# Self heads over fewer score banks: transposed scores on two PSUM banks, a value bank for each group, two buffers of reciprocals

## The reference, cut to what matters

```
# L0 and L3: gated memory
memory_proj = memory @ W_mem
attn = softmax(hidden @ memory_proj^T / sqrt(D));  context = attn @ memory_proj
gate = sigmoid([hidden, context] @ W_gate + b);    out = rmsnorm(hidden + gate * context)

# L1, self attention: the part that the change touches
x = rms_norm(hidden, ln_in_w)
mixed = where(vm, x @ v_qkv, x @ l_qkv)            # q, k, v: 16 heads of 16 features
q, k = apply_rotary(q, k, position_ids)
ctx = softmax(q k^T / 4, causal) @ v
hidden = hidden + where(vm, ctx @ v_dense, ctx @ l_dense)
...                                                # cross attention, experts
```

## Time and profile before

| | |
|---|---|
| median of 3 runs | 784.29 us (783.54 to 785.41) |
| the profiled execution | 783.74 us, its span 781.9 us |
| PE busy | 695.7 us (89%) |
| DVE, ACT, POOL busy | 408.9, 354.2, 107.1 us |
| mean granted TensorE clock | 0.938 |
| DMA | 34.55 MB, mean 44 GB/s |

### The profile page before, as it was taken

How to read it: one execution, slowest core, us unless ns; L and a number is a source line. 1 busy time by engine, 2 the same in 40 slices (tenths; PEclk the granted TensorE clock), 3 DMA queues, 4 the chain that set the end, 5 groups by cost and what they waited for, 6 DMA issues and landing times.

```text
span 781.9 us, 13323 instructions
## 1 busy us (share of the span) xinstructions
PE 695.7 (89%) x5560; PEld 547.7 (70%) x5560; DVE 408.9 (52%) x814; ACT 354.2 (45%) x702; POOL 107.1 (14%) x140
## 2 busy tenths in 40 slices
PE   7698898789999899999886969977899999999995
PEld 5576675547987677689774857754497967667984
DVE  2637826645764745252356394375655756443424
ACT  3503253466442466554253124524664335665424
POOL 0100000362000132300001000005700002332000
PEclk9989999688999999999997988987799999999998
DMA  7042000020103000050400020000220400000000
GB/s 287 20 178 81 2 2 29 1 75 21 55 21 142 1 2 1 1 189 1 168 27 1 1 81 2 2 28 1 75 74 2 156 7 1 1 2 1 1 0 28
DMA packets 6843, 34.55 MB, mean 44 GB/s; under 512 B 1536, under 2 KB 3072, under 8 KB 5248
## 3 DMA queue, kind: packets, MB, share of 16 engines
q1 hardware_dynamic: 5344, 26.85, 9.3%
q10 hardware_dynamic: 1440, 6.86, 2.4%
HBM read 32.66 MB, written 1.05 MB: 43 GB/s over the span
## 4 chain that ended last, share of the span: by engine, by line
PE 73%; DVE 18%; ACT 6%; issue 2%; DMA 0%; DVEq 0%; ACTq 0%; SPq 0%
PE ps_A L898 4%; PE ps_B L898 4%; PE ps_A L683 4%; PE ps_B L683 3%; PE ps_B L861 3%; PE ps_A L861 3%; PE ps_B L975 2%; PE ps_B L696 2%; PE ps_A L696 2%; PE ps_A L975 2%; DVE max_B L1620 2%; PE ps_A L1025 2%; PE ps_B L1025 2%; PE ps_A L1013 2%; PE ps_B L1013 2%; PE ps_A L649 2%
## 5 line engine op out<-in xcount | busy, mean ns | idle before, releaser
L1620 DVE TENSOR_REDUCE max_A<-ps_A 128x2 f32<-128x512 f32 x64 | 40.2, 685 | 21.6 <-PE ps_A L824 12.1
L1620 DVE TENSOR_REDUCE max_B<-ps_B 128x2 f32<-128x512 f32 x64 | 40.4, 685 | 20.3 <-PE ps_B L824 11.4
L544 POOL TENSOR_TENSOR xv_B<-big_B 128x256 f32<-128x256 f32 x24 | 18.5, 778 | 226.0 <-ACT big_B L1302 113.1
L544 POOL TENSOR_TENSOR xv_A<-big_A 128x256 f32<-128x256 f32 x24 | 17.6, 743 | 209.2 <-ACT big_A L1306 107.8
L861 PE MATMUL ps_B<-q_B,kz_B 64*128 64x256 f32 (+1 forms) x320 | 33.4, 315 | 7.2 <-ACT big_B L1306 4.0
L1137 ACT ACT_TABLE_LOAD x29 | 37.2, 1283 | 0.5
L861 PE MATMUL ps_A<-q_A,kz_A 64*128 64x256 f32 (+1 forms) x320 | 32.8, 315 | 5.0 <-ACT big_A L1306 4.2
L861 PEld LDWEIGHTS ps_B<-q_B,kz_B 64*128 64x128 f32 (+1 forms) x320 | 24.3, 197 | 17.6 <-ACT big_B L1306 7.0
L683 PE MATMUL ps_B<-q_B,kz_B 128*128 128x256 f32 x264 | 36.2, 299 | 0.5 <-DVE kz_B L1532 0.3
L683 PEld LDWEIGHTS ps_B<-q_B,kz_B 128*128 128x128 f32 x264 | 34.3, 202 | 2.6 <-issue 1.4
L683 PE MATMUL ps_A<-q_A,kz_A 128*128 128x256 f32 x264 | 35.1, 295 | 1.1 <-DVE q_A L1511 1.1
(11 more groups left out here) (379 smaller groups left out, 1693.2 us busy)
## 6 DMA issues: line engine op xcount, KB each, us to landing
ffn_w<-in_l1m SPq DMA_DIRECT2D x2, 3072.0 KB, 11.1
ffn_w<-in_l2f SPq DMA_DIRECT2D x2, 3072.0 KB, 10.7
attn_w<-in_l1a SPq DMA_DIRECT2D x2, 2048.0 KB, 10.5
v_B<-in_l1d ACTq DMA_DIRECT2D x2, 1408.0 KB, 6.1
v_A<-in_l1d ACTq DMA_DIRECT2D x2, 1408.0 KB, 5.9
attn_w<-in_l2q SPq DMA_DIRECT2D x2, 1024.0 KB, 5.2
attn_w<-in_l2q SPq DMA_DIRECT2D x4, 512.0 KB, 4.9
v_A<-in_gm SPq DMA_DIRECT2D x2, 512.0 KB, 5.0
```

The lines of the kernel that those rows point to most:

```text
L544: nc.gpsimd.tensor_tensor(L.key_sums(a, i), p[:, 0:S], p[:, S:2 * S], ALU.add)\
L1620: last = nc.vector.tensor_reduce(mx[:, :, h], L.ps[:, h % 4, :].rearrange("p (q k) -> p q k", q=ST), AX.X, ALU.max)
```

## The change

For self heads `SCORE_BANKS` goes from 3 to 2: a pair of transposed scores now waits for both exponentials of the pair before it. `value_bank` gives the first group bank 2 and the second bank 3, so that `busy` is 2 and no `weigh` waits for `head_out` of the group before. `recip` gives each group a half of `L.xn`. Beside that the table `ORDER` is another one for all four engines. The number of instructions is the same on every engine.

```diff
@@ ORDER @@
     "PE": [
-        2, 2, 2, 2, 1, 1, 1, 1, 2, 2, 1, 1, 2, 1, 1, 8, 6, 1, 1, 3, 1, 2, 1, 4, 2, 1, 1, 1, 2, 1, 1, 3, 2,
+        2, 2, 2, 2, 1, 1, 1, 1, 2, 2, 1, 1, 2, 1, 1, 8, 5, 1, 2, 3, 1, 2, 1, 2, 2, 2, 2, 1, 1, 1, 2, 1, 1,
...
@@ -421,14 +421,14 @@
-        SCORE_BANKS = [3, 3, 2]
+        SCORE_BANKS = [2, 3, 2]
 
         def value_bank(a, g):
 
-            return 2 + g % 2 if a == LATENT else 3
+            return 3 if a == CROSS else 2 + g % 2
 
         def recip(L, a, g):
-            return L.chunk(L.probs, g % 2) if a == LATENT else L.recip[:]
+            return L.chunk(L.probs, g % 2) if a == LATENT else L.chunk(L.xn, g) if a == SELF else L.recip[:]
@@ -880,7 +880,7 @@
-                        busy = 2 if a == LATENT else 1
+                        busy = 1 if a == CROSS else 2
```

More of the change, by code:

```diff
@@ L137 @@
     "PE": [
[10 rows of a table removed]
-    "ACT": [
[6 rows of a table removed]
-    "DVE": [
[6 rows of a table removed]
[10 rows of a table added]
+    "ACT": [
[6 rows of a table added]
+    "DVE": [
[6 rows of a table added]
     "POOL": [
-        0, 1, 2, 17, 16, 8, 8, 9, 9, 1, 17, 16, 8, 8, 8, 8],
+        0, 1, 2, 17, 16, 8, 8, 9, 9, 1, 11, 2, 2, 1, 2, 3, 2, 10, 8, 8, 8, 8],
 }
```

## The result

The changed kernel takes 804.49 us (median of 4 runs, 802.26 to 806.66) against 784.18 (783.54 to 785.41): ratio 1.027, 95% interval 1.024 to 1.030, 20.3 us slower. The forecast was 794.3 with a range up to 802. The sign was right, the size was not, and the time lies outside the range. The profiled execution took 806.66, its span is 804.9. The four executions stand in two pairs, 802.26 and 802.59 at a mean granted clock of 0.934, 806.38 and 806.66 at 0.922, and the profile is of the second pair.

What follows compares the result with a forecast made beforehand. The prediction took TensorE, busy 89% of the span, to bound the kernel. Its terms, 7.7 + 0.3 + 4.5 + 1.0 − 3.5 = +10.0 us, gave 793.7 for the profiled execution, 794.3 against the median, range 784 to 802.

Steps and rivals of the forecast that it cites:

- Value banks and reciprocals: Self heads' weigh and reciprocal: freed of waiting for head_out, where nothing was lost; gain 0, at most 0.3 us.
- The context load: Between the passes: PE reaches L592 sooner, but ctx_B lands no earlier behind ffn_w; 7.7 us of new idle.
- third rival: Between the passes: the small context load lands early, as ctx_A did, so no 7.7 us wait; 786.6 us, chance 0.08.
- Between the passes, the rest: Norms, rotary, clock and stacking between the passes, beside the load: sum +0.3 us, between −6 and +5.
- The rotary's 3.5: Between the passes: DVE does lane B's rotary between lane A's norms, so A's L664 waits; +3.5 us.
- the clock's 1.5: Between the passes: the long idle lets the clock fall, so one or two products more run at half rate; +1.5 us.
- The 2.3 of A's gated memory: Between the passes: DVE and ACT finish lane A's gated memory during the load's wait, so its waits go; −2.3 us.
- The second wait for the keys' casts: Between the passes: the lanes' stacking comes singly, giving a second wait like the one before; +2.9 us.
- Second pass, self attention: All 32 heads' maxima precede the first transposed scores, so DVE bounds the stage; +4.5 us, bounds −2 and +9.
- First pass, self attention: Two pairs of A's maxima ahead of B's last two delay B's first transposed scores; +1 us, −2 to +4.
- Cross and latent attention: Both passes: closer lanes put one's pairs over the other's 0.68 us waits; −3.5 us, bounds −7 and +2.
- second rival: Self attention: two score banks cost more than the order covers, half of 64 pairs uncovered, 14 us; 802.6 us, chance 0.11.

Runs made afterwards that it cites:

- e2: The changed kernel's banks (two for scores, value bank per group, two reciprocals) with the table ORDER of the kernel before; 787.03 us.
- e1: The changed kernel, with SyncE issuing lane B's context for the second pass ahead of the ffn_w load; 795.19 us.
- e8: The kernel before with two score banks for self heads alone, value bank, reciprocal and table as before; 788.73 us.
- e3: The kernel before with the new table ORDER alone, so three score banks, one value bank, one reciprocal; 807.10 us.
- e9: The kernel before, three score banks, with the new table up to the end of the first pass and the old one after; 789.30 us.
- e10: The kernel before, three score banks, with the new table throughout and lane B's context issued ahead of ffn_w; 792.70 us.
- e4: The changed kernel's banks, with the old table up to the end of the first pass and the new one after; 801.26 us.
- e6: The changed kernel's banks and the old table, with the new table only from the stacking before the second pass's self attention on; 799.09 us.
- e7: The changed kernel's banks, new table only from first pass's end to stacking of the second's self heads, lane B's context ahead of ffn_w; 802.28 us.
- e5: The changed kernel's banks, with the new table up to the end of the first pass and the old one after; 784.45 us.
- e11: The kernel before with the new table only up to the first steps of the first pass's self attention; 781.65 us.

## Why the prediction was wrong

By its steps, on the profiled executions (+23.0 us of span, forecast +10.0):

- **Value banks and reciprocals, 0.** Right; L898 doesn't wait for DVE in either kernel, and e2 shows no cost of its own for them.
- **The context load, 7.7.** Right in mechanism and size: 7.9 in the trace, and 7.2 to 9.3 with the half clock behind it by e1. The chance for the third rival (the load lands early) was rightly small, 11.1 us against 2.1.
- **Between the passes, the rest, +0.3.** Too small in the sum, 1.3 us more idle beside the load and 1.8 of clock, and right only in some of its parts. The rotary's 3.5 came as the 3.3 at L696, the clock's 1.5 as 1.8. A's norm waits went by 3.2 and B's grew, not the 5.3 that I credited. The 2.3 of A's gated memory did not go: L633 and L649 still wait 1.6, and L611 and L623 3.3 beside them. The second wait for the keys' casts (+2.9) did not come: there is one, now of lane B, 3.3 in place of 2.9.
- **Second pass, self attention, +4.5.** Measured 2.3 idle and 2.0 of clock, 4.3 in all. DVE bounds the maxima as said, but PE waits 5.8 us for them and not some 10, and the term had no clock in it. The near hit is partly luck.
- **First pass, self attention, +1.** Measured 1.5 idle and 1.4 of clock, but not for the reason given. The stage idles 10.8 to 11.0 us in every trace with two banks, with the old table too (e2, e8), and 9.2 to 9.8 in every trace with three, with the new table too (e3, e9, e10). So the idle is the banks' and not that of A's maxima put ahead.
- **Cross and latent attention, −3.5.** This is the step that failed, and with it the range. From the first cross attention to the experts' end and from the second to the end of the kernel the changed kernel idles 3.3 us more and loses 3.7 to the clock, +7.0 in place of −3.5: 10.5 of the 13 us missed. In e1, whose clock was the better, the same rows give 4.3 us more idle and 1.7 less of clock, still +2.6. I argued that closer lanes cover each other's waits for exponentials. They cover 0.7 us of them: in the two cross stages these waits came to 7.9 us before and 7.2 in the changed kernel. I had set the term from 24 us of idle without asking how much of it was such waits. What grew is waits for DVE. PE's waits in the first pass's cross stage, before (134 to 245 us) and changed (134 to 262 us):

```profile
PE ps_A L861 <- ACT big_A L1306: 2.5, 3, 1.1
PE ps_B L861 <- ACT big_B L1306: 1.1, 2, 0.7
PE ps_B L809 <- DVE max_B L1620: 0.7, 1, 0.7
PE ps_B L683 <- DVE q_B L1511: 0.2, 1, 0.2
```

```profile
PE ps_B L809 <- DVE max_B L1620: 2.8, 3, 1.7
PE ps_A L861 <- ACT big_A L1306: 2.6, 3, 1.2
PE ps_B L683 <- DVE q_B L1511: 2.0, 1, 2.0
PE ps_B L861 <- ACT big_B L1306: 0.9, 2, 0.7
```

The first of these, lane B's wait for its maxima, is the new table's: 2.6 to 2.8 us in all six traces that have it in the first pass, 0.7 or less in the ten others. The wait at L683 is not: it is 2.0 in e4, e6 and e8 with the old table, and 0.5 and 0.6 in e2 and e7, which run the same instructions up to there as e4 and e6.

And I read the granted clock of 0.79 in the earlier trace rows without pricing it. It says that 11 to 12 us of a cross stage are lost at half clock, as much as to idling, and this part moved: with the row under it 11.9 to 17.2 in the first pass, 12.1 to 10.5 in the second. In e1 the first is 11.4, with the same instructions, so most of this shift belongs to the execution and not to the order. Clock was in my sum as 1.5 us, between the passes alone; the runs show it in every stage that has waits.

One slip stands beside this: the two passes have 64 self heads, so 32 pairs and not 64 (the trace has 128 matmuls of L867, four to a pair). The bound of the banks is 32 × 0.44 = 14 us, and the second rival's term 7.

The two banks were in the sum with 1.5 us; e8 shows 5 under the old table and e10 against e1 2.6 under the new one. The second rival had the mechanism but not the size: neither its 14 us of waits came nor the 7 of the right count. The two pairs of executions bear on the range: the pair at 0.934 lies 0.3 and 0.6 us above its end of 802, the pair at 0.922 over 4, so the step was wrong in either, and the size of the miss depends on the pair.

How much of the changed kernel's 20.3 us is what: 7.2 to 9.3 the load (e1; the first at nearly equal clock), 2.6 the banks (e10 against e1), 8.4 to 9.6 the order beside them. Most of the order's loss, the load's included, arises from the end of the first pass on (e4 801.3, e5 784.5). How these last split stays open, since e6 and e7 could not separate the stages. The trace of e10, with neither the load nor the banks, has 2.9 us more than before between the passes and 3.1 in the second self stage (idle and clock); its first pass's cross stage has 9.1 more, 8 of it clock, but it is an execution at 0.926, 4 us above e10's median.

## What to carry to other kernels

When the order of an engine is rewritten, first list the loads whose issue hangs on a point in the program, and count what stands between that point and the first reader: here a load of 2 us was one of 11 behind a 3 MB one, and moving it ahead of that one was a change of a few lines. Before a term is set from a stage's idle time, list which waits make that idle: here a third of it was of the kind that the order could cover. Price the granted clock of each stage beside its idle time (busy by 1 less the clock), and treat a stage at 0.8 as one whose cost can move by several us between executions of the same instructions (5.8 us of clock's loss here). Compare executions at equal clock before a difference of under 1% is put down to the code, and look at the idle time beside it: e5 is faster than e2 by the medians and idles 7 us more.

## What the runs showed of the hardware that was not expected

The time of this kernel moves by several us with the granted clock alone. Of 71 executions of the kernel before, 4 took 778.3 to 779.0 at 0.946 and 67 took 781.2 to 785.8 at 0.934 to 0.942. The changed kernel and e1 run the same instructions up to the end of the first pass, and lost 26.4 and 20.3 us to the clock there. The kernel before and e9 idle 86.1 and 86.6 us, and e9's span is 5.2 us longer, with 6.4 more of clock's loss; e11's profiled execution of 780.05 lost 35.9 where before lost 40.5.

Waits move between executions of the same instructions too: L683 of lane B waited 0.5 us in e2 and 2.0 in e4. A delay of 0.7 us on one wait left three executions of eleven at 782.3 to 782.7 and eight at 786.3 or more. Which of two shifts falls on which side was not foreseen by anything in the traces, and remains open.
